# Adding the causal mask of an attention value pass with TensorE products in PSUM instead of GpSimd selects

## What is computed

```python
x = L0_attn_x
xn = _layernorm(x, axis=-1)
x = x + attn0(xn) + experts0(xn)          # 16 experts, top 2, and a shared one
xn = _layernorm(x, axis=-1)
x = x + delta_rule_attention(xn) + experts1(xn)   # 4 live experts, top 2

def attn0(x):                              # 16 heads of 8
    q, k, v = heads(Wq, bq), heads(Wk, bk), heads(Wv, bv)
    scores = einsum('bhqd,bhkd->bhqk', q, k) / 8 ** 0.5
    scores = where(key > query, -1e12, scores)
    return einsum('bhqk,bhkd->bhqd', softmax(scores), v) @ Wm + bm
```

## Time and profile before

| | |
|---|---|
| median of three runs | 1806.54 us (1803.79 to 1811.10) |
| span of the profiled execution, first to last instruction | 1759.6 us |
| what lies around the span: median less span | 46.9 us |
| TensorE busy, weight loads | 1587.2 us (90%), 1099.6 us (62%) |
| VectorE, ScalarE, GpSimd busy | 1401.9 (80%), 955.8 (54%), 915.0 us (52%) |
| fillers on TensorE | 936, busy 255.8 us |
| GpSimd's selects | 256, busy 169.8 us |

### The profile page before, as it was taken

How to read it: one execution, slowest core, us unless ns; L and a number is a source line. 1 busy time by engine, 2 the same in 40 slices (tenths; PEclk the granted TensorE clock), 3 DMA queues, 4 the chain that set the end, 5 groups by cost and what they waited for, 6 DMA issues and landing times.

```text
span 1759.6 us, 34071 instructions
## 1 busy us (share of the span) xinstructions
PE 1587.2 (90%) x12430; PEld 1099.6 (62%) x12430; DVE 1401.9 (80%) x2672; ACT 955.8 (54%) x1562; POOL 915.0 (52%) x973
## 2 busy tenths in 40 slices
PE   4899999889899999999989999999999999989950
PEld 2774555555566555445445877788888877778740
DVE  5779877677787878778796998888898899989942
ACT  2741556566666666555743556565555665535620
POOL 5207877651665475678776146622221365654256
PEclk9879999999999999999999999999999999999985
DMA  7963689989999776667448567665666577668413
GB/s 229 303 158 132 186 223 261 273 267 249 283 292 259 214 193 163 153 187 195 119 125 264 165 199 229 195 211 173 192 209 201 185 224 232 189 196 252 132 58 91
DMA packets 277959, 354.69 MB, mean 202 GB/s; under 512 B 32272, under 2 KB 204304, under 8 KB 272416
## 3 DMA queue, kind: packets, MB, share of 16 engines
q1 hardware_dynamic: 237600, 287.92, 57.1%
q0 software_dynamic: 17056, 33.66, 6.9%
q10 hardware_dynamic: 23136, 30.94, 5.1%
HBM read 197.48 MB, written 122.68 MB: 182 GB/s over the span
## 4 chain that ended last, share of the span: by engine, by line
PE 43%; DVE 23%; POOL 9%; issue 9%; DMA 7%; SPq 5%; ACT 4%; ACTq 0%; DVEq 0%; POOLq 0%
PE Y L1124 7%; PE R L867 5%; PE R L900 5%; PE R L869 5%; PE R L868 5%; POOL gat L1408 4%; DVE row_max L1997 3%; POOL xs_dram L1432 3%; DVE state L2098 3%; PE R L883 3%; PE Y L1018 2%; DMA q_rows<-kq 2%; DVE hid L2146 2%; DMA fw<-wf 2%; DVE dw L2092 1%
## 5 line engine op out<-in xcount | busy, mean ns | idle before, releaser
L1432 POOL DMA_INDIRECT xs_dram<-sc_in,pos x256 | 265.1, 1036 | 150.8 <-issue 58.7
L1408 POOL DMA_INDIRECT gat<-ys_dram,pos x256 | 262.6, 1026 | 125.3 <-issue 62.3
L1997 DVE TENSOR_REDUCE row_max<-R 128x6 f32<-128x768 f32 x256 | 238.9, 951 | 63.5 <-PE R L982 58.4
L900 PE MATMUL R<-ident_b 128*128 128x512 bf16 x936 | 255.8, 394 | 32.3 <-DVE K L1850 26.3
L1452 POOL TENSOR_TENSOR o_acc<-o_acc,read 128x512 f32<-128x512 f32 x112 | 146.1, 1304 | 263.8 <-DVE read L2108 262.7
L1124 PEld LDWEIGHTS Y<-fd,hid 128*128 128x128 f32 (+1 forms) x1824 | 232.3, 192 | 53.7 <-DVE hid L2146 25.9
L1604 ACT ACTIVATE probs<-R 128x768 f32<-128x768 f32 x256 | 203.8, 809 | 105.4 <-PE R L1006 99.2
L1124 PE MATMUL Y<-fd,hid 128*128 128x128 f32 (+1 forms) x1824 | 249.9, 280 | 11.3 <-DVE hid L2146 10.7
L1443 POOL TENSOR_SCALAR_AFFINE_SELECT probs<-probs 128x512 f32<-128x512 f32 x256 | 169.8, 664 | 158.1 <-ACT probs L1604 155.1
L867 PE MATMUL R<-fhl,fw 128*128 128x512 f32 x418 | 182.2, 436 | 1.3 <-DVE fhl L2136 1.3
L1723 ACT ACTIVATE sil<-R 128x512 f32<-128x512 f32 x190 | 112.9, 596 | 127.9 <-PE R L869 83.3
(11 more groups left out here) (270 smaller groups left out, 3399.6 us busy)
## 6 DMA issues: line engine op xcount, KB each, us to landing
fw<-wf SPq DMA_DIRECT2D x38, 1408.0 KB, 7.8
q_rows<-kq SPq DMA_DIRECT2D x128, 256.0 KB, 5.1
fx<-xs_dram SPq DMA_DIRECT2D x86, 256.0 KB, 3.4
xs_dram<-gat SPq DMA_DIRECT2D x24, 512.0 KB, 4.9
qk_dram<-qk_parts SPq DMA_DIRECT2D x32, 384.0 KB
Q<-qk_dram SPq DMA_DIRECT2D x64, 192.0 KB
K<-qk_dram SPq DMA_DIRECT2D x64, 192.0 KB
fw<-wf SPq DMA_DIRECT2D x96, 128.0 KB
```

The lines of the kernel that those rows point to most:

```text
L900: pe.matmul(psum["R"][:, b * C:(b + 1) * C], ident_b[:, :], ident_b[:, :].unsqueeze(1).to_broadcast([P, TILES, P]), start=True, stop=True)
L1408: pool.indirect_dma_start(gat[:, i % 2, 2 * t + a, :], None, ys_dram[l][g], bass.IndirectOffsetOnAxis(ap=pos[l][g][a][:, col:col + 1], axi ...
L1432: pool.indirect_dma_start(xs_dram[g], bass.IndirectOffsetOnAxis(ap=pos[l][g][a][:, col:col + 1], axis=0), sc_in[:, n % 2, t * P:(t + 1) * ...
L1997: dve.tensor_reduce(row_max[:, b, h2, :, :], pair[:, :].rearrange("p (g c t) -> p g c t", g=2, t=P)[:, :, 0:3, :], AX.X, ALU.max).then_inc ...
```

## The change

B2 leaves its accumulation open and adds the mask in PSUM: four products of 64 rows and 128 columns per head pair, with `causal_h` as weights and `ident_h` as the moving side. Both tiles exist already, for B1. The exponential then gives zeros above the diagonal. The select, its semaphore and GpSimd's part of B2 are gone; BP waits for ScalarE's release of the scores' bank. In the scheduler's table, B2's assumed TensorE length goes from 0.36 to 0.5 and its GpSimd length goes away, and so the order of all engines is worked out anew. C1b, which overwrites `x1n`, now waits for the previous chunk's transposes by name (`xT1` filled), in the table and on ScalarE.

```diff
@@ table()
-                stage(t, "B2", n, k, after=[(("BM", n, b, "SP"), 2.4)], PE=0.36,
-                      ACT=(0.7, [("BP", *divmod(i - 2, NPAIR // 2), "PE")] if i >= 2 else []), POOL=0.68)
+                stage(t, "B2", n, k, after=[(("BM", n, b, "SP"), 2.4)], PE=0.5,
+                      ACT=(0.7, [("BP", *divmod(i - 2, NPAIR // 2), "PE")] if i >= 2 else []))
                 banks("B2", n, k, ("B2", n, k, "ACT"), 2)
                 if k % 2:
-                    after = [("B2", n, k - 1, "POOL"), ("B2", n, k, "POOL"), ("Q4", n, 0, "ACT")]
+                    after = [("B2", n, k - 1, "ACT"), ("B2", n, k, "ACT"), ("Q4", n, 0, "ACT")]
                     stage(t + 1, "BP", n, k // 2, after=after, PE=0.8)
...
-            stage(t + 16, "C1b", n, after=[("C1", n, 0, "POOL")], DVE=0.1, ACT=2.1)
+            stage(t + 16, "C1b", n, after=[("C1", n, 0, "POOL")], DVE=0.1, ACT=(2.1, since(n, 1, ("C2", 0, "PE"))))
@@ TensorE, B2 and BP
                     for g, bank in enumerate(banks):
                         pe.matmul(bank[:, 0:3 * P].rearrange("p (c t) -> p c t", t=P)[:, 0:3:2, :],
-                                  key[g][:, q0:q0 + P], q[g][:, q0:q0 + S], start=True, stop=True)
+                                  key[g][:, q0:q0 + P], q[g][:, q0:q0 + S], start=True, stop=False,
+                                  skip_group_check=True)
                     for g, bank in enumerate(banks):
-                        ins = pe.matmul(bank[:, P:2 * P], key[g][:, q0 + P:q0 + S], q[g][:, q0 + P:q0 + S],
-                                        start=True, stop=True)
+                        pe.matmul(bank[:, P:2 * P], key[g][:, q0 + P:q0 + S], q[g][:, q0 + P:q0 + S],
+                                  start=False, stop=False, skip_group_check=True)
+                    for j in range(2):
+                        cols_j = slice(64 * j, 64 * j + 64)
+                        for g, bank in enumerate(banks):
+                            rows = slice(64 * g, 64 * g + 64)
+                            ins = pe.matmul(bank[:, 0:2 * P].rearrange("p (c t) -> p c t", t=P)[:, :, cols_j],
+                                            causal_h[rows, j, 0, :],
+                                            ident_h[rows, j, cols_j].unsqueeze(1).to_broadcast([64, 2, 64]),
+                                            start=False, stop=j == 1, skip_group_check=True)
                     ins.then_inc(pair.full, 1)
...
-                            wait(*probs_masked(n, 2 * k + c // 2 + 1))
+                            wait(*bank_of["st", n, 2 * k + c // 2].released())
@@ GpSimd
-                if kind == "B2":
-                    pool.wait_ge(*bank_of["st", n, k].released())
-                    c = 2 * (k % 2)
-                    diag = probs[:, (k // 2) % 2, c:c + 2, 0:2 * P]
-                    pool.affine_select(out=diag, in_=diag, compare_op=ALU.is_ge, fill=0.0, base=0,
-                                       pattern=[[0, 2], [0, 2], [1, P]], channel_multiplier=-1)\
-                        .then_inc(probs_masked.sem, 1)
@@ ScalarE, C1b
                     if n >= 1:
                         wait(*x1n_saved(n - 1))
+                        wait(*bank_of["xT1", n - 1].filled())
```

More of the change, by code:

```diff
@@ L812, in two_layer_kernel @@
         max_split = signal("max_split")
-        probs_masked, values_weighted = signal("probs_masked", NPAIR), signal("values_weighted", 2 * GROUPS)
+        values_weighted = signal("values_weighted", 2 * GROUPS)
         b3_loaded, acc_saved = signal("b3_loaded", 2, 16), slots("acc_saved")
```

## The result

The changed kernel takes **2043.5 us** (median of 4, 2033.1 to 2049.0) where the kernel before takes 1806.1 on the same chip (4 runs): a ratio of **1.131**, 95% interval 1.127 to 1.135. It is slower by 237 us. The prediction said 1792.

The account below looks back on a forecast made before the run. TensorE was taken as the bound in the last stage, with room in the attention turned into fillers. Masks +37.1, fillers -45.3 and the selects' wait -6.3 gave -14.5 us: 1806.5 becomes 1792 us, range 1771 to 1819.

Parts of the forecast that it names:

- the one on the selects: Attention: 256 selects of 0.664 us leave GpSimd, by themselves costing nothing; only a TensorE wait is paid.
- the slower one: Rival, attention: mask products stay on the path at 0.33 us per four, +32.9 us, 1839 us; chance 0.12.
- One sign: Attention: TensorE idle well above the present 54 us would show the forecast wrong, the fillers being only a mark.
- The masks: Attention: four added mask products per pair take 0.145 us of TensorE, times 256: +37.1 us, between 28.9 and 84.5.
- The fillers: TensorE's list: 185 fewer in the attention, 53 fewer in the turn, 30 more afterwards, at 0.218 us each: -45.3 us.
- The fillers were only a mark: Rival, attention: other engines and loads set the pace, so masks hide and removed fillers give nothing back: 1804.7 us; chance 0.28.
- The selects' wait: Attention: TensorE's wait for the select ahead of V's product goes, -6.3 us, bounds 0 and 15.9.
- The turn: Stage between the attention and what follows: 53 fewer fillers on TensorE, -11.6 us, counted within the -45.3.
- The later fillers: After the turn: 30 more fillers on TensorE, +6.5 us, counted within the -45.3.
- VectorE is freed: Rival, first layer's sums of gathered rows: faster without selects beside them, up to 12.2 us, 1780 us; chance 0.14.
- Span and median: Whole kernel: the 46.9 us between profiled span 1759.6 and median 1806.5 lie outside the program's instructions and stay.

Follow-up runs that it names:

- e2: Kernel before with its old lists, mask products added on TensorE, GpSimd's selects and its waits on ScalarE removed: 2024.2 us.
- e1: Kernel before with only the 1,024 mask products added on TensorE; lists, fillers and GpSimd's selects kept: 1808.5 us.
- e13: Kernel before with mask products, spare selects, no GpSimd waits on ScalarE, and each chunk's eight scatters or gathers moved directly behind one another: 2039.5 us.
- e6: Kernel before with its old lists, mask products, no GpSimd wait on ScalarE, and two spare selects per pair in place of the select: 1814.8 us.
- e9: Kernel before with mask products added, selects kept, and the planner told 0.5 us of TensorE for B2 (828 fillers for 936): 1820.9 us.
- e10: Kernel before with only the planner's TensorE time for B2 raised from 0.36 to 0.5 us (828 fillers for 936): 1810.9 us.
- e16: Kernel before with one spare select behind each scatter or gather that another directly follows (163 places): 1795.8 us, ratio 0.998.
- e17: Kernel before with one spare select behind each scatter or gather that stands between two others (96 places): 1799.2 us, ratio 0.999.
- e8: Changed kernel with two spare selects (0.75 us) on GpSimd behind each scatter and gather of the attention: 1882.3 us.
- e12: Changed kernel with one spare select (0.37 us) on GpSimd behind each scatter and gather of the attention: 1857.1 us.
- e11: Changed kernel with every scatter, and every gather of the first layer, cut from 128 rows to 64: 2041.0 us.

## Why the prediction was wrong

**The step that failed** is the one on the selects: "By themselves they cost nothing, because TensorE hides them with other stages". It asked what the selects' time hides and not what the selects keep apart. The numbers were in front of it: a select shortens the gap ahead of the next scatter but puts the two scatters 1.94 us apart, and GpSimd's wait of 155 us for ScalarE paced its queue. The prediction read both as slack. Taken out, the transfers come 1.26 us apart, and TensorE's signals reach VectorE and ScalarE late, by up to 26 us after V's products; TensorE then waits for them in turn. Two pairs of runs price that: e2 less e1 is 216 us (231 less 15.5), e13 less e6 is 216 (237 less 21), of a loss of 237. No rival had it; the slower one was about the masks. One sign was named and came true: TensorE idle in the attention far above 54 us, 280. But it was said to mean that the fillers were only a mark.

**The masks**, +37.1: measured 10 to 15.5, under the lower bound of 28.9. From e9 less e10 and e1 less before. The Trainium skill's rule on overhead ("TensorEngine Tiling (Array Packing)", Performance Considerations), by which the prediction estimated 80 us, is further off.

**The fillers**, -45.3: there are 728 of them with 200.7 us busy, as forecast, and nothing came back. e10, with 108 fewer, is 17 us slower where the price of 0.218 us gives 23.5 faster; TensorE's gaps in its attention are 101 us (75 in e1, which has the old lists), its granted clock 0.93 (0.97). "The fillers were only a mark" had the better half of this, though a mark would have cost nothing.

**The selects' wait**, -6.3: gone, and a like one stands in its place, as a sentence of the prediction feared: V's product now waits for the exponential.

```profile
PE Y L1027 <- ACT probs L1606: 18.4, 5, 9.1
```

**The turn**, -11.6: measured -13.3 (31.5 for 44.8). **The later fillers**, +6.5: +1.8. Right in mechanism, small beside the rest.

**VectorE is freed**, -12.2 at most: not tried by itself. VectorE's busy time in the attention is 552.7 for 584.7 us, but in a stage of 1041 us it is idle for nearly half the time.

**Span and median.** The prediction put 46.9 us between them "outside the program's instructions". In every run since, span and own time differ by at most 2.7 us (2031.4 and 2033.1 for the change). The profiled execution of the kernel before was simply faster, by some 2%, than the timed ones (1791 to 1811 in six jobs). Part of what the other runs' attention has over its 751 us comes from that, and they are better compared with one another: against e16 and e17, level with the kernel before in time, the changed attention is 254 to 260 us longer. Why it was faster is open. It is, with e8's, the only trace without a late wait, while e1, with the same list on GpSimd, has 58 us of them; that the timed executions had such waits too is likely, but no trace of them is there to show it.

## What to carry to other kernels

Before taking work off an idle-looking engine, ask what that work keeps apart and what its waits pace: list what the engine will issue next, and how closely. If GpSimd is left with nothing but indirect transfers, keep other work, or a wait on a slower engine, between them (here 0.35 us took most of the loss away and 0.12 us nothing), without letting its queue grow so long that others wait for it, as in e8. Look for stretches in which all engines stand still while only GpSimd issues, and for waits that the profile calls remote on one core. And price fillers, or any instruction that a plan has put into expected waits, by a run that changes their number alone; here their own length gave not even the sign.

## What the runs showed of the hardware

While GpSimd issues rows of indirect transfers 1.26 us apart, semaphores that TensorE raises rise late, up to 26 us after V's products in the changed kernel. VectorE and ScalarE wait for them, and TensorE for those two, though in these stalls none of them waits for the transfers. At 1.52 us apart the late waits are 156 us (e12), at 1.91 there are none (e8). No remote wait of any run is for a semaphore that VectorE or ScalarE raises. The Trainium skill ("DMA: Bandwidth & Descriptors", SWDGE vs HWDGE vs iDMA) says that for such transfers software on GpSimd computes the descriptors and writes them into rings in SBUF; e11, with half the rows per transfer, shows hardly any dependence on the rows, neither in GpSimd's time (0.96 us for 1.01) nor in the loss.

A long row is not needed. In e1, whose GpSimd has its selects, VectorE's maximum waits for products of line 982 that end at 463.45, behind three gathers:

```profile
461.02 0.99 POOL L1417 DMA_INDIRECT gat<-ys_dram,pos  x1 [0.23 <-issue]
...
462.31 0.96 POOL L1417 DMA_INDIRECT gat<-ys_dram,pos  x1 [0.30 <-issue]
...
463.12 0.33 PE L982 MATMUL R<-causal_h,ident_h 64*128 64x256 bf16 x4
...
463.58 0.94 POOL L1417 DMA_INDIRECT gat<-ys_dram,pos  x1 [0.30 <-issue]
...
465.39 0.96 DVE L2006 TENSOR_REDUCE row_max<-R 128x6 f32<-128x768 f32 x1 [3.47 <-remote]
```

Nor is a row always harmful. The profile of the kernel before has a row of 16 ahead of its attention and one of 17 in its turn, 46 us together, in which TensorE is idle for 3 us; its four rows of six and seven inside the attention have under 1 us. But no signal is late anywhere in that one execution, so its rows do not tell how close or how long a row may be. And in the changed kernel's last stage this row of six leaves TensorE without a gap:

```profile
1804.35 0.98 POOL L1417 DMA_INDIRECT gat<-ys_dram,pos  x1
1805.63 0.94 POOL L1417 DMA_INDIRECT gat<-ys_dram,pos  x1 [0.30 <-issue]
...
1808.25 1.27 POOL L1417 DMA_INDIRECT gat<-ys_dram,pos  x1 [0.30 <-issue]
1809.83 0.94 POOL L1417 DMA_INDIRECT gat<-ys_dram,pos  x1 [0.30 <-issue]
1811.08 0.94 POOL L1417 DMA_INDIRECT gat<-ys_dram,pos  x1 [0.30 <-issue]
```

So the distance counts, and within a row the harm grows, but something else counts too, and what it is stays open. What in the chip holds up TensorE's signals while GpSimd issues was not tried.
